# A post-norm block with differential attention and routed experts: a table of two places per step, statistics among a batch's projections, and routed up products turned round

## The chip, the core and the metric

The kernel runs on one core of a Trainium2 chip. The core has five engines that work side by side and meet at semaphores: TensorE (PE, with its weight loads shown apart as PEld), VectorE (DVE), ScalarE (ACT), GpSimd (POOL) and SyncE (SP, which here only issues DMAs). The metric is the device time of one execution in microseconds, lower is better.

## What is computed

The input is four sequences (batches) of 512 tokens of 256 values. Two layers follow each other, each added to its input and normed:

```python
x = _layernorm(x + _L0_attn_ref(x, ...), axis=-1)
x = _layernorm(x + _L0_ffn_ref(x, ...), axis=-1)
```

The attention has 16 heads over 4 key/value groups, each with two score maps under a causal mask; the second softmax is subtracted from the first with a factor lambda. Its output goes through a group norm over a whole batch and is projected:

```python
a1 = _softmax(s1); a2 = _softmax(s2)
diff = a1 - lam * a2
out = jnp.einsum('bhts,bhsd->bhtd', diff, v).transpose(0, 2, 1, 3)
mean = jnp.mean(out, axis=(1, 3), keepdims=True)
var = jnp.var(out, axis=(1, 3), keepdims=True)
out = (out - mean) * jax.lax.rsqrt(var + EPS)
...
return out @ Wo
```

The feed-forward layer picks one of 8 experts for each token (top 1, sigmoid gate), and adds a shared expert:

```python
h = _silu_mul(xs @ wg)      # 256 -> 2 x 512
o = h @ wd                  # 512 -> 256
```

## The kernel before

All of it is written by hand for each engine; the order of instructions on an engine is the order of the code, and semaphores (`wait_ge`) join the engines.

**Attention steps.** A batch b is worked in `body(b, ...)` through 40 steps, the list `STEPS` of (qt, g, kt): 128 queries of tile qt, group g, 128 keys kt. PE writes the scores of a step into a ring of three PSUM banks (`scores`, L950), ACT takes their exponentials (L1178), POOL masks the step where kt equals qt (L1317, 16 such steps a batch: steps 0, 1, 2, 3, 5, 7, 9, 11, 14 and so on), and PE multiplies them with the values one step later (`weigh`, L964). After the last step of a unit (one qt and g) ACT copies the sums out (L1196), PE turns them (task `norm`, L881) and DVE divides and combines them (L1430 to L1433). Beside that PE works "banks" of scores (`score_bank`, L803 and L804) from which DVE takes each row's maximum (L1405); task `mt` turns the finished maxima (L877), and SP carries them into the rows that later scores read.

**The next batch is prepared inside the running one.** `prep` on PE turns x (L787) and projects it into q and k (L791), ACT copies the products out (L1088). POOL then rotates and splits them into three bf16 parts, 18 operations a batch in the list `PREP` (lines 538 to 547), with two casts a pair on ACT (L1102, L1105). `PREP_LATER` (batch 0: `PREP_FIRST`) names the step at which POOL issues each. SP stores the parts and loads them back in stacked form.

**The layer behind attention** for batch b runs among the steps of batch b + 1, as tasks. `TASKS[n]` lists what each engine does at the end of step n; ACT and POOL do them one step later in their own order, behind that step's exponentials or mask. Group norm has the tasks `mean`, `square`, `sum_squares`, `var`; each of four token tiles then has `turn`, `project`, `x2`, `retake`, `logits` (steps 6 + 5 qt on); routing has `top`, `choose`, `gate`, `rank`, `ids`; the shared expert has twelve tasks in steps 28 to 39. `BOUNDARY` stands between two batches: values (`v`, L873), the last `norm` and `sum`. The 8 `prep` of the next batch come at the start of `body`. For the last batch there is nothing to prepare, and what follows its attention is `TAIL`.

**Routed experts.** Tokens are sorted by expert into 23 tiles of 128 rows (`NROUTE`). For each, POOL gathers rows by an indirect DMA, PE turns them (L1026), multiplies with the expert's up weights (L1042: tokens are the stationary side, 512 columns of weights stream, four products), ACT and DVE make the hidden rows, PE turns those (`turn_hidden`, L1050, four 128 by 128 transposes) and ACT copies them (L1251), and PE multiplies with the down weights (L1061). All eight experts' weights (1.5 MB each) lie in SBUF, loaded from body 3 on (`load_experts`), and the expert of a tile selects an address by a register (`owner_of`, L1031).

## Time and profile before

| | us |
|---|---|
| median of 3 runs | 854.79 |
| lowest, highest | 852.37, 856.72 |
| profiled execution, its own time | 854.18 |
| its span, first to last instruction | 852.4 |
| PE busy in the span | 755.7 |
| DVE, ACT, POOL busy | 463.6, 330.5, 305.2 |

The span differs from the profiled execution's own time by 1.8 us at its two ends. The trace gives each instruction's start from the start of the span, its duration, and the idle time of its engine ahead of it with what ended it. Batch 0 has its steps from 73 us, batch 1 its boundary from 190.5, batch 2 from 360.1, batch 3 from 532.7, `TAIL` begins at 638.5, the routed tiles at 703. An instruction's end on PE is modelled and includes the time until its result is out, so groups of matmuls are better read by the distance of their starts.

### The profile page before, as it was taken

The numbers are of one execution on the slowest core, as the hardware profiler recorded it, in microseconds if no ns is written. First come the engines' busy times: TensorE is split into PE (matmuls) and PEld (weight loads), VectorE is DVE, ScalarE is ACT, GpSimd is POOL, SyncE is SP. The second block draws the span as 40 slices with busy tenths as digits, with TensorE's granted clock in tenths as the row PEclk, the third lists the DMA queues.
The fourth block names the chain that finished last, engine by engine and source line by source line (L and its number), as shares of the span: only waits on it lengthen the run. The fifth ranks groups of instructions, "written<-read, shape, count | busy, mean of one in ns | idle before, by whom it ended". The sixth has DMA issues, their size and how long they took to land.

```text
span 852.4 us, 10350 instructions
## 1 busy us (share of the span) xinstructions
PE 755.7 (89%) x3430; PEld 369.7 (43%) x3430; DVE 463.6 (54%) x1040; ACT 330.5 (39%) x607; POOL 305.2 (36%) x263
## 2 busy tenths in 40 slices
PE   7488899997699989977999899889999799999994
PEld 3243334333244433532444334434326555666662
DVE  2766986751667775416677655566425342333332
ACT  2414544434465433154554232554663002222220
POOL 3057511122982012029821130221240034666653
PEclk9778999999899999996899899999999999999998
DMA  3695085002038210020272100700067012221100
GB/s 128 149 335 149 5 197 88 28 2 38 0 70 178 41 55 3 22 42 1 63 161 41 55 4 2 210 2 1 2 207 293 25 44 63 60 60 62 46 22 1
DMA packets 51748, 62.95 MB, mean 74 GB/s; under 512 B 11303, under 2 KB 42797, under 8 KB 49840
## 3 DMA queue, kind: packets, MB, share of 16 engines
q1 hardware_dynamic: 42992, 49.29, 23.4%
q0 software_dynamic: 3824, 6.83, 2.7%
q10 hardware_dynamic: 4880, 6.16, 2.3%
q8 instruction: 29, 0.48, 0.2%
q14 instruction: 23, 0.19, 0.1%
HBM read 42.59 MB, written 22.41 MB: 76 GB/s over the span
## 4 chain that ended last, share of the span: by engine, by line
PE 71%; DVE 10%; POOL 6%; issue 4%; DMA 4%; ACT 2%; SPq 1%; POOLq 0%; DVEq 0%; ACTq 0%
PE pv_ps L964 15%; PE wide_ps L1042 9%; PE wide_ps L950 7%; PE s_ps L803 7%; PE wide_ps L791 5%; DVE mneg L1405 4%; PE wide_ps L934 4%; PE s_ps L835 3%; PE wide_ps L906 3%; PE s_ps L804 3%; PE pv_ps L1061 2%; PE misc L1061 2%; PE misc L881 2%; DMA k_parts<-w_exp 2%; PE wide_ps L939 2%
## 5 line engine op out<-in xcount | busy, mean ns | idle before, releaser
L1405 DVE TENSOR_REDUCE mneg<-s_ps 128x1 f32<-128x384 f32 (+3 forms) x352 | 216.7, 638 | 98.9 <-PE s_ps L804 94.9
L1178 ACT ACTIVATE w_exp<-wide_ps 128x512 f32<-128x512 f32 x320 | 180.0, 599 | 120.6 <-PE wide_ps L950 118.8
L964 PE MATMUL pv_ps<-w_exp,work 128*64 128x512 f32 x640 | 180.5, 644 | 10.0 <-POOL w_exp L1317 8.0
L1317 POOL TENSOR_SCALAR_AFFINE_SELECT w_exp<-w_exp 128x1024 f32<-128x1024 f32 x64 | 70.8, 1106 | 287.1 <-ACT w_exp L1178 287.1
L803 PE MATMUL s_ps<-w_exp 96*128 96x256 bf16 (+3 forms) x512 | 131.6, 316 | 20.7 <-DVE mneg L1405 13.2
L950 PE MATMUL wide_ps<-w_exp 98*128 98x512 bf16 x320 | 124.5, 398 | 13.2 <-ACT w_exp L1178 11.9
L950 PEld LDWEIGHTS wide_ps<-w_exp 98*128 98x128 bf16 x320 | 31.9, 103 | 155.5 <-ACT w_exp L1178 98.4
L804 PE MATMUL s_ps<-mask,identb 128*128 128x128 bf16 (+2 forms) x352 | 89.6, 254 | 0.0
L1042 PE MATMUL wide_ps<-w_exp,tables 128*128 x184 | 82.8, 592 | 0.0
L803 PEld LDWEIGHTS s_ps<-w_exp 96*128 96x128 bf16 x512 | 46.2, 101 | 70.9 <-DVE mneg L1405 43.0
L1196 ACT COPY work<-pv_ps 128x512 f32<-128x512 f32 x64 | 37.5, 585 | 58.1 <-PE pv_ps L964 57.2
L964 PEld LDWEIGHTS pv_ps<-w_exp,work 128*64 128x64 f32 x640 | 32.7, 138 | 54.3 <-issue 37.3
L791 PE MATMUL wide_ps<-work,tables 128*128 128x512 f32 x96 | 49.9, 677 | 6.9 <-ACT work L1088 6.9
L1623 DVE TENSOR_TENSOR work<-work,wide_ps 128x512 f32<-128x512 f32 x23 | 15.8, 688 | 70.8 <-PE wide_ps L1042 70.8
L1042 PEld LDWEIGHTS wide_ps<-w_exp,tables 128*128 128x128 f32 x184 | 33.2, 190 | 33.0 <-issue 33.0
L804 PEld LDWEIGHTS s_ps<-mask,identb 128*128 128x128 bf16 x352 | 36.0, 102 | 22.7 <-issue 4.1
L881 PE MATMUL misc<-ident,work 128*128 128x128 f32 x256 | 40.8, 284 | 2.8 <-ACT work L1158 2.0
L1251 ACT COPY work<-s_ps 128x512 f32<-128x512 f32 x23 | 13.5, 585 | 74.9 <-PE s_ps L1050 68.9
L1430 DVE RECIPROCAL rl<-misc 128x8 f32<-128x8 f32 x64 | 12.8, 200 | 50.5 <-PE misc L881 50.5
L1370 POOL DMA_INDIRECT out<-work,rows_of x23 | 23.6, 1024 | 40.5 <-DVE work L1631 38.5
L1297 POOL TENSOR_TENSOR rstd<-mv,halfneg 128x1 f32<-128x1 f32 x16 | 9.0, 562 | 80.7 <-DVE mv L1471 80.7
L934 PE MATMUL wide_ps<-x2T,w_sh 128*128 128x512 f32 x64 | 34.3, 663 | 1.4 <-DVE place L1534 1.4
(164 smaller groups left out, 982.5 us busy)
## 6 DMA issues: line engine op xcount, KB each, us to landing
w_exp<-q_parts SPq DMA_DIRECT2D x96, 128.0 KB, 5.0
w_exp<-w_up_in SPq DMA_DIRECT2D x8, 1024.0 KB, 8.9
slot_tokens<-x ACTq DMA_DIRECT2D x1, 4864.0 KB, 20.8
work<-x_in SPq DMA_DIRECT2D x8, 512.0 KB, 7.2
w_exp<-w_down_in SPq DMA_DIRECT2D x8, 512.0 KB, 9.6
q_parts<-w_exp SPq DMA_DIRECT2D x6, 512.0 KB, 6.0
w_exp<-k_parts SPq DMA_DIRECT2D x18, 128.0 KB, 3.7
gated_rows<-work SPq DMA_DIRECT2D x4, 512.0 KB
```

Of the source, the lines that this page charges most:

```text
L791: last = nc.tensor.matmul(slot, wqk_sb[:, c, pair, half, :], xT[:, c, :], start=(c == 0), stop=(c == DC - 1))
L803: nc.tensor.matmul(o[:, n], q_stack[0:KROWS, qt, hs, :], keys[0:KROWS, hs // 4, 0:qt + 1, :], start=(n == 0), stop=False)
L804: last = nc.tensor.matmul(o[:, :, w - P:w], identb[:], mask[:].unsqueeze(1).to_broadcast([P, len(rows), P]), start=False, stop=True)
L881: last = nc.tensor.transpose(here[:, r * P:(r + 1) * P], ol[:, arg % 2, r * P:(r + 1) * P], ident[:])
L934: last = nc.tensor.matmul(here[:], w_sh[:, ch * 2 * F + at:ch * 2 * F + at + P], x2T[:, ch, :], start=(ch == 0), stop=(ch == DC - 1))
L950: nc.tensor.matmul(st_bank(v), k_stack[0:MROWS, b % 2, gs, kt, :], q_stack[0:MROWS, qt, gs * 4:gs * 4 + 4, :], start=True, stop=True).then ...
L964: last = nc.tensor.matmul(pv_ps[s * 64:(s + 1) * 64, :], vo[:, kt, g, :], probs[:, n % NP, s, :], start=(kt == 0), stop=(kt == qt))
L1042: last = nc.tensor.matmul(up_ps[:, r, half, :], xeT[:, r, ch, :], w, start=(ch == 0), stop=(ch == DC - 1))
L1178: nc.scalar.activation(probs[:, n % NP, s], st_bank(v), ACT.Exp, scale=float(DH) ** -0.5).then_inc(st_done, 1)
L1196: nc.scalar.copy(ol[:, u % 2], pv_ps[:]).then_inc(pv_done, 1)
L1317: nc.gpsimd.affine_select(out=e, in_=e, compare_op=ALU.is_ge, fill=0.0, base=0, pattern=[[0, 8], [1, P]], channel_multiplier=-1).then_inc( ...
L1405: nc.vector.tensor_reduce(out=mneg[:, qt, rows[0]:rows[-1] + 1], in_=s_ps[:, (v - 1) % 2, 0:len(rows) * w].rearrange("p (r k) -> p r k", r ...
```

## The change

1. **Two places per step.** `TASKS[n]` becomes `TASKS[n, half]`. A task at MID stands on PE between the two halves of a step's banks, ahead of `weigh(n - 1)`; on DVE between the halves; on ACT and POOL it comes in its own step n, behind the exponentials or mask, and no longer one step later. The table is written out anew, place by place: the first tile's `turn` stands at step 3 (before: 6), the second tile's tasks at steps 9 to 12 (before: 11 to 15), routing at 22 to 26 (27 and 28), the shared expert at 25 to 38 (28 to 39). `var`'s ACT part becomes a task `scale` in two halves, `square` too.
2. **The front of a batch.** The 8 `prep` move from the start of `body` into `BOUNDARY`, and `mean`, `square` and the `sum_squares` stand among them. Batch 3 has no `prep`; its boundary keeps the statistics. POOL's `PREP_LATER` and `PREP_FIRST` move to later steps; `bank_table` is spread a little differently.
3. **Routed tiles.** The up product's sides are exchanged: weights are stationary (sixteen products of 128 by 128 by 128 a tile), the tokens stream, and the result is the hidden matrix already turned. `turn_hidden`, `hid`, ACT's `take_hidden` and two semaphores go; DVE writes `hidT` directly.
4. **A ring for up weights.** Only the eight down matrices (0.5 MB each) stay in SBUF. The up weights (1 MB) are loaded for each of the 23 tiles into a ring of four, by SP, which reads the tile's owner into a register; slot i is loaded when `up(i - 4)` is done. POOL gathers the rows of tiles 2 and 3 ahead of the rows to be added.

```diff
-    here = [(2, 0, 8), (3, 8, 19)] if first else [(3, 3, 19)]
-    for back, rows in ((0, here), (-1, [(0, 19, 22), (1, 22, 28), (2, 28, 40)])):
+    here = [(2, 0, 9), (3, 9, 18)] if first else [(3, 2, 20)]
+    for back, rows in ((0, here), (-1, [(0, 20, 22), (1, 22, 28), (2, 28, 39)])):
...
-TASKS[0].append(("mean", 0, 1))
-TASKS[4].append(("var", 0, 1))
...
+put(1, END, ("var", 0, 1))
+put(3, END, ("norm", 1, 0), ("scale", 0, 1), ("scale", 1, 1), ("turn", 0, 1))
+put(9, MID, ("turn", 1, 1))
+put(9, END, ("project", 1, 1))
...
-BOUNDARY = [("v", 0, 0), ("norm", NUNIT - 1, 1), ("sum", QT - 1, 1)]
+BOUNDARY = [("v", 0, 0), ("prep", 0, 0), ("prep", 1, 0), ("norm", 15, 1), ("prep", 2, 0), ("prep", 3, 0), ("sum", 3, 1), ("mean", 0, 1),
+            ("prep", 4, 0), ("square", 0, 1), ("sum_squares", 0, 1), ("sum_squares", 1, 1), ("prep", 5, 0), ("square", 1, 1), ("prep", 6, 0), ("prep", 7, 0), ("sum_squares", 2, 1), ("sum_squares", 3, 1)]
...
-PREP_FIRST = [-4, -4, -3, -3, -2, -1, -1, -1, 0, 1, 2, 3, 3, 4, 4, 5, 6, 7]
-PREP_LATER = [0, 0, 1, 1, 2, 3, 3, 4, 4, 5, 6, 6, 7, 8, 8, 9, 10, 11]
+PREP_FIRST = [-4, -4, -3, -3, -2, -1, -1, -1, 1, 2, 2, 4, 5, 6, 6, 7, 8, 8]
+PREP_LATER = [1, 3, 3, 3, 4, 5, 5, 6, 6, 7, 7, 7, 9, 10, 10, 11, 13, 14]
...
+            def load_upper(i):
+
+                if i >= RINGUP:
+                    sp.wait_ge(up_full, 2 * (i - RINGUP + 1))
+                e = sp.value_load(owner[0:1, i:i + 1], min_val=0, max_val=E - 1)
+                sp.dma_start(w_upper[:, i % RINGUP], w_up.rearrange("e k n -> (e k) n")[bass.ds(e * D, D)].rearrange("(c p) n -> p c n", p=P)
+                             ).then_inc(upper_loaded[i % RINGUP], 16)
...
                 for half in range(2):
-                    for ch in range(DC):
-                        w = w_exp[:, bass.ds(e * WEXP + ch * 2 * F + half * F, F)]
-                        last = nc.tensor.matmul(up_ps[:, r, half, :], xeT[:, r, ch, :], w, start=(ch == 0), stop=(ch == DC - 1))
+                    for fc in range(F // P):
+                        for ch in range(DC):
+                            w = w_upper[:, i % RINGUP, ch, half * F + fc * P:half * F + (fc + 1) * P]
+                            last = nc.tensor.matmul(up_ps[:, r, half, fc * P:(fc + 1) * P], w, xeT[:, r, ch, :], start=(ch == 0), stop=(ch == DC - 1))
                     last.then_inc(up_full, 1)
```

Three places of the order of instructions follow. The first is POOL (GpSimd) at the front of batch 1. L1317 is the mask of a diagonal step; L538, L540, L542, L544, L546, L547 are cos, sin, even, odd, rest and low of a pair; in the changed kernel the lines are L1348 for the mask, L578 to L587 for the six, L1324 and L1325 for the group norm's scale and L1328 for a tile's deviation. Before:

```order
L538 TENSOR_TENSOR work<-w_exp,tables 128x1024
L540 TENSOR_TENSOR rot_sin<-w_exp,tables 128x1024
L1317 AFFINE_SELECT w_exp<-w_exp 128x1024
L542 TENSOR_TENSOR w_exp<-work,rot_sin 128x512
L544 TENSOR_TENSOR w_exp<-rot_sin,work 128x512
L1317 AFFINE_SELECT w_exp<-w_exp 128x1024
L538 TENSOR_TENSOR work<-w_exp,tables 128x1024
L1317 AFFINE_SELECT w_exp<-w_exp 128x1024
L540 TENSOR_TENSOR rot_sin<-w_exp,tables 128x1024
L546 TENSOR_TENSOR w_exp<-w_exp 128x1024
L542 TENSOR_TENSOR w_exp<-work,rot_sin 128x512
L544 TENSOR_TENSOR w_exp<-rot_sin,work 128x512
```

The row ahead of these is batch 1's first mask. Now, from the same mask on:

```order
L1348 AFFINE_SELECT w_exp<-w_exp 128x1024 x3
L578 TENSOR_TENSOR work<-w_exp,tables 128x1024
L1348 AFFINE_SELECT w_exp<-w_exp 128x1024
L1324 TENSOR_TENSOR head_scale<-head_var,halfneg 128x4
L1325 TENSOR_TENSOR head_scale<-head_scale,gw 128x4
L1348 AFFINE_SELECT w_exp<-w_exp 128x1024
L580 TENSOR_TENSOR rot_sin<-w_exp,tables 128x1024
L582 TENSOR_TENSOR w_exp<-work,rot_sin 128x512
L584 TENSOR_TENSOR w_exp<-rot_sin,work 128x512
L578 TENSOR_TENSOR work<-w_exp,tables 128x1024
L1348 AFFINE_SELECT w_exp<-w_exp 128x1024
L1328 TENSOR_TENSOR rstd<-mv,halfneg 128x1
```

The four masks of steps 0 to 3 stood between pairs of preparation; now one preparation and the scale stand between them, and the rest comes behind.

The second is PE (TensorE) at the boundary of batch 1: values (L873, now L926), preparation (L787 and L791, now L840 and L844), `norm` (L881, now L934), `mean` (L890, now L943), `var` (L894, now L947), scores (L950, now L1003). Before:

```order
L873 MATMUL misc<-wv_sb,work 128x128 x8
L881 MATMUL misc<-ident,work 128x128 x4
L787 MATMUL wide_ps<-ident,work 128x128 x8
L791 MATMUL wide_ps<-work,tables 128x512 x12
L950 MATMUL wide_ps<-w_exp 128x512 x5
L890 MATMUL wide_ps<-head_tot,averager 128x16 x4
L950 MATMUL wide_ps<-w_exp 128x512
L964 MATMUL pv_ps<-w_exp,work 64x512 x2
```

Now:

```order
L926 MATMUL misc<-wv_sb,work 128x128 x8
L840 MATMUL wide_ps<-ident,work 128x128 x8
L934 MATMUL misc<-ident,work 128x128 x4
L844 MATMUL wide_ps<-work,tables 128x512 x4
L943 MATMUL wide_ps<-head_tot,averager 128x16 x4
L844 MATMUL wide_ps<-work,tables 128x512 x8
L1003 MATMUL wide_ps<-w_exp 128x512 x6
L1017 MATMUL pv_ps<-w_exp,work 64x512 x2
L1003 MATMUL wide_ps<-w_exp 128x512
L947 MATMUL wide_ps<-averager,work 128x1 x4
```

`mean` has moved from behind the first five scores to the middle of the projections, and `var` from step 4 to step 1.

The third is PE in a routed tile, from the register load of its owner (L1031, now L1084) on: hidden rows turned (L1050), gathered rows turned (L1026, now L1079), up products (L1042, now L1097), down products (L1061, now L1108). Before:

```order
L1031 TENSOR_LOAD tables
L1031 ISA x2
L1050 MATMUL s_ps<-ident,work 128x128 x4
L1026 MATMUL s_ps<-ident,work 128x128 x2
L1042 ISA
L1042 MATMUL wide_ps<-w_exp,tables 128x512
L1042 ISA
L1042 MATMUL wide_ps<-w_exp,tables 128x512
```

Now:

```order
L1084 TENSOR_LOAD tables
L1084 ISA x2
L1079 MATMUL s_ps<-ident,work 128x128 x2
L1097 MATMUL wide_ps<-tables,w_exp 128x128 x16
L1108 ISA
L1108 MATMUL pv_ps<-w_exp,work 128x256
```

The four transposes are gone, sixteen short products stand for four long ones, and no address is worked out for them.

## Rows read from the trace of the kernel before

**Rows 1.** Stages: busy us (count) of PE, PEld, DVE, ACT, POOL; clock, DMA share, GB/s:

```profile
206.50:256.00 49.50, 38.16 (x178) 16.38 (x178) 29.38 (x57) 29.03 (x53) 44.52 (x29) 0.90 0.14 32
376.00:428.00 52.00, 41.56 (x182) 17.09 (x182) 32.49 (x58) 29.78 (x54) 44.58 (x29) 0.80 0.13 31
482.00:532.70 50.70, 49.52 (x203) 21.73 (x202) 25.34 (x55) 14.54 (x26) 9.53 (x8) 0.94 0.06 17
```

**Rows 2.** Timeline, POOL, front of batch 1: start, us, engine, line, what [idle before]:

```profile
207.78 1.09 POOL L1317 TENSOR_SCALAR_AFFINE_SELECT w_exp<-w_exp 128x1024 f32<-128x1024 f32 x1 [21.51 <-ACT w_exp L1178]
...
244.41 0.54 POOL L1297 TENSOR_TENSOR rstd<-mv,halfneg 128x1 f32<-128x1 f32 x1 [3.51 <-DVE mv L1471]
...
252.75 1.09 POOL L1317 TENSOR_SCALAR_AFFINE_SELECT w_exp<-w_exp 128x1024 f32<-128x1024 f32 x1
```

**Rows 3.** Timeline, POOL, front of batch 2: its first and its eighth mask:

```profile
377.39 1.09 POOL L1317 TENSOR_SCALAR_AFFINE_SELECT w_exp<-w_exp 128x1024 f32<-128x1024 f32 x1 [24.68 <-ACT w_exp L1178]
...
424.12 1.08 POOL L1317 TENSOR_SCALAR_AFFINE_SELECT w_exp<-w_exp 128x1024 f32<-128x1024 f32 x1
```

**Rows 4.** Groups by line and shape: count, busy us, mean ns, idle us before:

```profile
L546 POOL TENSOR_TENSOR w_exp<-w_exp 128x1024 f32<-128x1024 f32 x9 | 19.3, 2146 | 0.4 <-ACT w_exp L1102 0.4
L547 POOL TENSOR_TENSOR w_exp<-w_exp 128x1024 bf16<-128x1024 f32 x9 | 19.4, 2160 | 1.5 <-ACT w_exp L1105 1.2
...
L1042 PEld LDWEIGHTS wide_ps<-w_exp,tables 128*128 128x128 f32 x184 | 33.2, 190 | 33.0 <-issue 33.0
```

**Rows 5.** Timeline, PE, batch 1: its waits for maxima, gate and routing:

```profile
288.95 0.23 PE L877 MATMUL misc<-identb,msplit 128*128 128x128 bf16 x1 [0.92 <-DVE o L1431]
...
309.00 0.34 PE L803 MATMUL s_ps<-w_exp 96*128 96x384 bf16 x1 [2.16 <-DVE mneg L1405]
...
310.27 1.14 PE L934 MATMUL wide_ps<-x2T,w_sh 128*128 128x512 f32 x1 [0.73 <-DVE place L1534]
...
357.13 0.22 PE L877 MATMUL misc<-identb,msplit 128*128 128x128 bf16 x1 [1.18 <-DVE msplit L1412]
```

**Rows 6.** Timeline, front of batch 3: statistics and two waits of PE:

```profile
538.00 1.04 PE L890 MATMUL wide_ps<-head_tot,averager 128*128 128x16 f32 x8 [0.17 <-DVE head_tot L1438]
...
539.07 2.61 DVE L1443 TENSOR_TENSOR work<-work,wide_ps 128x512 f32<-128x512 f32 x4 [1.22 <-PE wide_ps L890]
...
541.77 2.19 ACT L1121 ACTIVATE work<-work 128x512 f32<-128x512 f32 x4 [0.87 <-DVEq L1449]
...
544.50 0.39 PE L950 MATMUL wide_ps<-w_exp 98*128 98x512 bf16 x1 [1.61 <-ACT w_exp L1178]
...
558.39 0.39 PE L950 MATMUL wide_ps<-w_exp 98*128 98x512 bf16 x1 [2.36 <-ACT w_exp L1178]
```

**Rows 7.** The chain that ended last, in one routed tile: start, us, what:

```profile
721.59 0.44 PE s_ps L1050 x4
722.02 0.22 PE s_ps L1026 x2
722.24 3.43 PE wide_ps L1042 x8
725.67 1.73 PE pv_ps L1061 x8
```

**Rows 8.** Timeline: the eight 128x128x128 products of `v`, batch 1, and their loads:

```profile
190.45 2.05 PE L873 MATMUL misc<-wv_sb,work 128*128 128x128 f32 x16
190.45 1.86 PEld L873 LDWEIGHTS misc<-wv_sb,work 128*128 128x128 f32 x16 [0.81 <-DVE mT L1425]
```

**Rows 9.** Timeline, PE: its first instruction among the routed tiles:

```profile
703.80 0.43 PE L1026 MATMUL s_ps<-ident,work 128*128 128x128 f32 x2 [1.52 <-issue]
```

**Rows 10.** Stages as in rows 1: while experts load, and among routed tiles:

```profile
641.00:656.00 15.00, 15.00 (x60) 8.42 (x59) 7.93 (x15) 7.19 (x15) 1.25 (x2) 1.00 1.04 384
730.00:780.00 50.00, 50.00 (x192) 31.63 (x191) 18.82 (x51) 12.06 (x25) 31.09 (x35) 1.00 0.20 60
```

**Rows 11.** DMA issues by line: count, KB of one, median us to landing:

```profile
w_exp<-w_up_in SPq DMA_DIRECT2D x8, 1024.0 KB, 8.9
```

More of the change, by code:

```diff
@@ new lines @@
+put(23, MID, ("choose", 0, 1))
+put(24, MID, ("mt", 0, -1))
+put(24, END, ("rank", 0, 1), ("ids", 0, 1))
+put(25, MID, ("shared_gate", 0, 1), ("ids", 1, 1))
+put(25, END, ("norm", 11, 0), ("shared_up", 0, 1))
+put(26, MID, ("gate", 0, 1))
+put(26, END, ("sum", 2, 0))
+put(27, MID, ("shared_gate", 1, 1))
+put(27, END, ("shared_up", 1, 1))
+put(29, MID, ("mt", 1, -1), ("shared_gate", 2, 1))
+put(29, END, ("norm", 12, 0), ("ids", 2, 1))
+put(30, MID, ("ids", 3, 1))
+put(31, MID, ("shared_up", 2, 1))
```

214 lines of the change are left out of this document (111 added, 103 removed).

## The prediction

> **What bounds the kernel now.** I read the stages first, then on each engine the timeline of those where PE is not full, and last the chain. PE is busy for 755.7 of the span's 852.4 us, so a gain comes from three sources only: gaps of PE, time at a lower clock, and PE work itself. The longest gaps lie at the front of batches 1 and 2 [rows 1]: in 206.5 to 256 PE is busy 38.2 of 49.5 us and POOL 44.5, in 376 to 428 PE 41.6 of 52 and POOL 44.6, at a granted clock of 0.90 and 0.80 (a mean of stretches at 2.4 and at 1.2 GHz). POOL sets the pace there: each diagonal step needs its mask from POOL before `weigh`, and POOL reaches the mask only after the preparation queued ahead. From the first mask to the eighth (step 11) POOL takes 252.75 - 207.78 = 44.97 us in batch 1 [rows 2], with one wait of 3.51 for the first tile's variance, and 46.73 in batch 2 [rows 3]. Behind that PE is nearly full, but for waits on DVE [rows 5]. Among the routed tiles PE has no gap: a tile is 0.44 + 0.22 + 3.43 + 1.73 = 5.82 us [rows 7], 23 tiles are 134.
>
> **Batch fronts, POOL's queue.** Now 17 of the 18 preparations stand ahead of the eighth mask; in the change 15 do, since low of pair 1 (step 11), rest and low of pair 2 (13 and 14) come behind it, and only the last was behind it before. That takes out one rest and one low, 2.15 + 2.16 = 4.3 us [rows 4]. The wait of 3.5 should go, since `project` of the first tile stands at step 4 and POOL asks for its variance only in step 5, behind cos of pair 1. The second tile's power is added (0.54) [rows 2]; the scale's two operations are ahead of it in both. The loop through ACT (odd, cast, rest, cast, low) leaves a step or more between each pair of them, so I see no new wait of POOL that is long. Gain: 4.3 + 3.5 - 0.5 = **7.3**, of which my walk through the four early masks gives back 0.3, as mask 1 waits for step 1's exponentials: **7.0** in batch 1. Batch 2 spends 1.8 more over the same queue (46.7 against 45.0), from late statistics, and these now come early: 7.0 + 1.6 = **8.6**. It is only gained if ACT and PE deliver the exponentials in time: in that stage PE's work of 38 us would have to fit in some 41, so the cover is thin.
>
> **Work moved into that stage.** The second tile's `project` (as long as L1061, 1.73 [rows 7]) and `retake` (two transposes, 0.22) now stand ahead of step 12's `weigh`, where PE waits anyway. 2.0 a batch: **4.0**. `mean` goes the other way, into the projections (1.0 us of PE), but PE now has values, a wait for ACT and the projections in an order that hides `norm` 15 behind preparation's transposes, which I set equal. ACT's squares (2.2 us) fit between its copies.
>
> **Waits further on.** In batch 1 these are 0.92 (maxima, `mt` 0), 2.16 (maxima queued on DVE behind routing and gate), 0.73 (`rank`) and 1.18 (`mt` 2), together 5.0 [rows 5]; batch 2 has the same four within 0.05 each. The new table puts `mt` 0 and 2 a step half or more behind their last bank and spreads top, choose, rank and gate over steps 22 to 26. I leave 0.5: 4.5 a batch, **9.0**. In the last third of batch 2 the clock is 0.94 of full [rows 1], 50.7 x 0.06 = 3.0 us lost; without such gaps ahead of it most comes back: **2.5**. A table with more places also makes waits of its own, which no row shows: a MID task stands ahead of `weigh` and of the next score, so whatever it waits for holds both. Between nothing and the 5.0 a batch that it takes away I put 1.5 a batch, nearer to nothing because each chain of a tile has a full step between its links: **+3.0**.
>
> **Batch 0.** It loses two `mt` waits of about 1 us, as in [rows 5], and gets one back (`mt` 2 of batch 0 now follows its last bank in the same step); low of pair 2 stands before the mask of step 9 and waits for a cast that ACT makes after step 9's exponentials, some 1 to 2 us. I take **0**, from -2 to +3.
>
> **Batch 3** has no projections to hide the statistics behind. `mean` starts at 538.0 when DVE's sum is there, in both; but the five scores ahead of it now come later, and ACT must do the squares before the first exponential: 539.07 + 2.61 for the deviations, then 2.19 of squares [rows 6] is 543.9, where before six exponentials were done. PE waits about 1.9 ahead of `mean` and 4.9 behind it, where it had 1.61; the 2.36 for the scale [rows 6] goes, since the variance comes three steps earlier. 1.9 + 4.9 - 1.6 - 2.4 = 2.8, less smaller waits of that stage: **+2.0**.
>
> **Routed tiles.** The transposes of the hidden rows go: -0.44. The up product keeps its streaming: 16 products of 128 columns are as many columns as 4 of 512. What may grow is the distance of starts. Products of this very shape stand in `v`: 16 halves (each float32 product is recorded as two) whose loads start (1.86 - 0.19)/15 = 0.111 us apart [rows 8]; by the matmuls' own row (2.05 - 0.28)/15 = 0.118, with the first, slow one in it. 32 halves at 0.1115 are 3.57 against 3.43, at 0.118 3.78. I take 3.57: the tile is 3.57 + 1.73 + 0.22 = 5.52, and 23 x 0.29 = 6.7. The first turn waits 1.52 for a register load among others [rows 9]; that load now comes later, behind other work: 0.9. Together **7.6**, between 2.8 (0.118) and 8.
>
> The Trainium skill speaks against this ("TensorE: Matmul & The Clock Gate", Part 3, The mechanism): it says that a weight load overlaps a running matmul only when the two use different row groups, and here all use all rows. By that rule loads would stand in line with the streams, the second rival below. In [rows 8] sixteen loads of one row group pass in 1.86 us beside 2.05 us of matmuls, so the trace does not bear it out; the same page's Part 2 (LDWEIGHTS) gives 128/1.2 = 107 ns a load, near the 0.111 seen.
>
> **The ring.** 1 MB a tile is 1.05 MB in 5.52 us, 190 GB/s, beside gathers of 60 GB/s that stretch little; 250 in all. While experts load the core moves 384 GB/s with PE full and undisturbed [rows 10]. The first load is issued when owners are known, more than 10 us ahead of PE's first need, the others up to three tiles ahead. Cost 0. SP's register reads and the small loads of row numbers now queue behind 1 MB loads, 2.7 us each at 384 GB/s; gathers have two tiles of slack.
>
> **Sum.** Against the profiled execution: 854.2 - 7.0 - 8.6 - 4.0 - 9.0 - 2.5 + 3.0 + 0 + 2.0 - 7.6 = **820.5**. The median of before is 0.6 above that execution, which I neglect.
>
> **Rivals.**
> - *The front does not move.* Masks come no earlier because ACT's casts and exponentials wait on each other and PE cannot deliver: the 15.6 and 4.0 stay away: 840. For it: PE's 38 us in 41; ACT's cast of a pair stands in order ahead of the next exponentials. Against: ACT is busy 29 of 49.5 us.
> - *Weight loads exposed.* Each half costs its load of 0.190 [rows 4] beyond its stream of 0.107 (3.43/32): 9.5 against 3.57, 23 x 5.9 = +137: 957. It cancels the whole sum from 33.7/23 = 1.5 us a tile on, 0.046 a half.
> - *The ring starves PE* (slower). A 1 MB load took 8.9 us to land [rows 11]. If loads came one after another at that pace, the tile is 8.9: 23 x 3.4 = +78: 898. It decides from 5.52 + 33.7/23 = 7.0 us a tile. For it: 23 MB where 8 were, one queue with the row numbers. Against: those 8.9 us were with others in flight, at 384 GB/s together [rows 10].
> - *Better than summed*: no new waits, the clock stays up in the fronts too: 5 to 12 less, 812.
>
> **Chances.** Forecast 0.55 (its own range 813 to 829), front unmoved or half moved 0.24, better 0.12, ring 0.06, loads 0.03. The first three reach from 808 to 842; that holds 8 in 10. About 0.5% (4.3 us) is what a measurement can tell from no change: faster 0.89, within 0.02 (the far end of the second case), slower 0.09, all of it from the ring and the loads.
>
> **What would show it.** The eighth mask of batch 1 38 us after the first (now 45), of batch 2 the same; no wait over 0.5 us before `mt` and the shared expert; batch 3's front with one gap of about 5 us ahead of its second group of scores; starts of the up halves 0.11 apart and a tile of 5.5 us; the DMA at about 250 GB/s among the tiles. It is wrong if PE waits for `upper_loaded` or for gathered rows, if POOL waits for casts, or if DVE, which now has the second tile's tasks among the banks of the last query tile, becomes what PE waits for.

## The result, and the profile after

The changed kernel takes **825.39 us** (median of 4 runs, 822.43 to 826.78) where the kernel before takes 853.58 beside it; the ratio is 0.967 (95% interval 0.9635 to 0.9711). The forecast was 820.5, range 808 to 842. So 28.2 us of the 33.7 that were summed did come. The profiled execution has a span of 825.1 us, 27.3 below that of the kernel before.

The page of the changed kernel begins so (busy time of each engine; among the lines on 40 slices the granted clock of PE):

```profile
PE 740.3 (90%) x3890; PEld 407.1 (49%) x3890; DVE 471.5 (57%) x1040; ACT 316.6 (38%) x584; POOL 308.1 (37%) x263
...
PEclk9878999999989999999999998799999999999997
```

To see where the time went, cut both traces at the same pieces of work: `v` of each batch (the boundary's first product), the first product of the last shared expert's tail, the first turn among the routed tiles, the end of the last down product. In us:

| stage | before | after | difference | forecast |
|---|---|---|---|---|
| head, to batch 0's `v` | 20.99 | 20.48 | -0.5 | 0 |
| batch 0 | 169.46 | 167.92 | -1.5 | 0 |
| batch 1 | 169.62 | 158.74 | -10.9 | -12.0 |
| batch 2 | 172.58 | 158.42 | -14.2 | -16.1 |
| batch 3, to the tail's start | 106.38 | 110.90 | +4.5 | +2.0 |
| tail, to the first routed turn | 64.77 | 66.01 | +1.2 | -0.9 |
| routed tiles, to the last product's end | 137.10 | 129.86 | -7.2 | -6.7 |
| what follows it | 11.5 | 12.7 | +1.2 | 0 |
| span | 852.4 | 825.1 | -27.3 | -33.7 |

(The forecast of batch 1 is 7.0 + 2.0 + 4.5 less half of the 3.0 for new waits, of batch 2 8.6 + 2.0 + 4.5 + 2.5 less the other half.)

**Fronts.** Timeline of POOL in batch 1: its first two masks (of steps 0 and 1), the second tile's deviation (rstd), the eighth mask, and low of pair 2:

```profile
205.34 2.14 POOL L1348 TENSOR_SCALAR_AFFINE_SELECT w_exp<-w_exp 128x1024 f32<-128x1024 f32 x2 [19.79 <-ACT w_exp L1216]
...
242.47 0.55 POOL L1328 TENSOR_TENSOR rstd<-mv,halfneg 128x1 f32<-128x1 f32 x1 [2.33 <-DVE mv L1501]
...
245.47 1.15 POOL L1348 TENSOR_SCALAR_AFFINE_SELECT w_exp<-w_exp 128x1024 f32<-128x1024 f32 x1
...
256.33 2.13 POOL L587 TENSOR_TENSOR w_exp<-w_exp 128x1024 bf16<-128x1024 f32 x1 [3.39 <-ACT w_exp L1149]
```

(In the order of instructions above, the three masks ahead of cos are these two and the last one of batch 0.) The eighth mask comes 245.47 - 205.34 = 40.1 us after the first, where it was 45.0 [rows 2]; the forecast was 38. The difference is about the wait of 2.33 for the second tile's variance, which the forecast had at nothing. That wait is not fixed: with the same order of instructions it is absent in the traces of e6 and e9 below, where the eighth mask comes 37.74 us after the first, while e12 has 40.86. In batch 2 it is 39.05 (46.73 before, [rows 3]). PE's longest wait in the front of batch 1, for a mask, has nearly gone. Before, and now:

```profile
214.60 1.81 PE L964 MATMUL pv_ps<-w_exp,work 128*64 128x512 f32 x4 [3.97 <-POOL w_exp L1317]
```

```profile
206.49 1.08 PE L1017 MATMUL pv_ps<-w_exp,work 128*64 128x512 f32 x4 [0.37 <-POOL w_exp L1348]
```

The stages of [rows 1] read now (PE, PEld, DVE, ACT, POOL busy; clock, DMA share, GB/s):

```profile
204.00:254.00 50.00, 41.07 (x201) 18.58 (x202) 30.40 (x57) 28.39 (x52) 43.93 (x30) 0.93 0.13 28
362.50:412.50 50.00, 41.66 (x204) 19.01 (x203) 30.87 (x57) 28.63 (x52) 43.87 (x30) 0.93 0.14 30
455.00:505.50 50.50, 49.87 (x234) 22.51 (x231) 31.78 (x66) 17.20 (x31) 9.61 (x7) 1.00 0.08 24
```

PE has more to do per us than before (41.1 of 50 where it was 38.2 of 49.5), and batch 2's last third is at full clock, where it was at 0.94. Of PE's remaining waits in batch 1, the two longest and the last:

```profile
228.28 0.61 PE L1003 MATMUL wide_ps<-w_exp 98*128 98x512 bf16 x1 [3.45 <-ACT w_exp L1216]
...
245.82 0.41 PE L964 MATMUL wide_ps<-ident,x 128*128 128x128 f32 x2 [2.11 <-DVE x L1506]
...
276.90 0.40 PE L856 MATMUL s_ps<-w_exp 96*128 96x128 bf16 x4 [0.63 <-DVE mneg L1435]
```

The third is the last one of the batch over 0.3 us: the four waits of [rows 5], 5.0 us, are gone from batches 1 and 2. The first two belong to the front, as do one of 1.34 and one of 0.71.

**Batch 3.** Timeline of its front, PE, DVE and ACT:

```profile
510.90 1.86 PE L943 MATMUL wide_ps<-head_tot,averager 128*128 128x16 f32 x8 [1.96 <-DVE head_tot L1468]
...
512.80 2.60 DVE L1473 TENSOR_TENSOR work<-work,wide_ps 128x512 f32<-128x512 f32 x4 [2.04 <-PE wide_ps L943]
...
515.49 2.19 ACT L1165 ACTIVATE work<-work 128x512 f32<-128x512 f32 x4 [7.26 <-DVEq L1479]
...
518.22 1.58 PE L1003 MATMUL wide_ps<-w_exp 98*128 98x512 bf16 x3 [4.18 <-ACT w_exp L1216]
519.96 1.97 PE L1017 MATMUL pv_ps<-w_exp,work 128*64 128x512 f32 x4 [0.16 <-POOL w_exp L1348]
```

PE waits 1.96 ahead of `mean` and 4.18 behind it, 6.1 where [rows 6] has 0.17 + 1.61 + 2.36 = 4.1: the 2.0 of the forecast. What is not in it is the clock: `mean` takes 1.86 where it took 1.04 [rows 6], and four halves of `weigh` 1.97 where they take 1.08 at 2.4 GHz (from 528.88 on). The granted clock is 0.50 from 510.96 to 528.0, 17.1 us; before it fell, PE had waited 0.68 and 1.96 us. In the kernel before, batch 3 has two stretches of 3.4 us at that level.

**Routed tiles.** PE at their start, and a tile of the chain that ended last (start, us, what):

```profile
682.47 0.41 PE L1079 MATMUL s_ps<-ident,work 128*128 128x128 f32 x2 [1.66 <-DMA work<-gated_rows,rows_of]
683.43 0.41 PE L1079 MATMUL s_ps<-ident,work 128*128 128x128 f32 x2 [0.55 <-ACT tables L1277]
683.68 3.74 PE L1097 MATMUL wide_ps<-tables,w_exp 128*128 128x128 f32 x32
689.15 0.44 PE L1079 MATMUL s_ps<-ident,work 128*128 128x128 f32 x2 [1.73 <-DMA work<-gated_rows,rows_of]
```

```profile
722.49 0.22 PE s_ps L1079 x2
722.71 3.57 PE wide_ps L1097 x32
726.28 1.73 PE pv_ps L1108 x8
```

A tile is 0.22 + 3.57 + 1.73 = 5.52, as summed, against the 5.82 of [rows 7]; 32 halves take 3.57 at 0.1116 apart. The first turn waits about as long as in [rows 9], now for gathered rows and not for a register. The third waits 1.73, since its gather could start only when the first turn had freed one of the two buffers. Stage 730 to 780, to be held against the second of [rows 10], and the ring's loads:

```profile
730.00:780.00 50.00, 50.00 (x384) 47.70 (x383) 19.79 (x54) 8.99 (x19) 33.49 (x37) 1.00 0.73 252
```

```profile
w_exp<-w_up_in SPq DMA_DIRECT2D x23, 1024.0 KB, 5.5
```

252 GB/s, and PE waits for no load of the ring.

**The end** is 1.2 us longer because the last two down products now follow each other directly; the last one used to wait 0.76 us for a copy by ACT, behind the transposes. The last two tiles' results therefore reach DVE and POOL together. POOL's last power of -0.5 waits for the scatter of the tile ahead:

```profile
810.44 1.89 PE L1108 MATMUL pv_ps<-w_exp,work 128*128 x8
...
812.94 0.42 DVE L1673 TENSOR_TENSOR work<-pv_ps,work 128x256 f32<-128x256 f32 x1
...
813.87 1.04 POOL L1400 DMA_INDIRECT out<-work,rows_of  x1 [1.29 <-DVE work L1666]
...
814.94 0.57 POOL L1395 TENSOR_TENSOR out_rstd<-out_mv,halfneg 128x1 f32<-128x1 f32 x1
...
816.78 1.03 POOL L1400 DMA_INDIRECT out<-work,rows_of  x1 [1.26 <-DVE work L1666]
```

From the product's end (812.33) to the start of the last scatter are 4.45 us; before, 3.24.

### The profile page after: what moved, and what is told of

Same layout as the page of the kernel before. It is cut to its first block, busy times and chain, and to the rows that moved or that the text cites. A ratio compares the mean times of both kernels' runs of the same rounds, so it can differ in the third digit from the quotient of the medians.

```text
span 825.1 us, 11250 instructions
## 1 busy us (share of the span) xinstructions
PE 740.3 (90%) x3890; PEld 407.1 (49%) x3890; DVE 471.5 (57%) x1040; ACT 316.6 (38%) x584; POOL 308.1 (37%) x263
## 4 chain that ended last, share of the span: by engine, by line
PE 69%; DVE 13%; POOL 6%; issue 5%; DMA 3%; ACT 2%; SPq 1%; POOLq 0%; DVEq 0%; ACTq 0%
PE pv_ps L1017 16%; PE wide_ps L1097 10%; PE s_ps L856 7%; PE wide_ps L1003 7%; DVE mneg L1435 6%; PE wide_ps L844 5%; PE wide_ps L987 3%; PE s_ps L888 3%; PE s_ps L857 3%; PE wide_ps L959 3%; PE misc L1108 2%; PE pv_ps L1108 2%; PE misc L934 2%; POOL w_exp L1348 2%; PE wide_ps L992 2%
## 5 line engine op out<-in xcount | busy, mean ns | idle before, releaser
L1017 PE MATMUL pv_ps<-w_exp,work 128*64 128x512 f32 x640 | 176.7, 633 | 3.0 <-ACT work L1234 1.9
L1348 POOL TENSOR_SCALAR_AFFINE_SELECT w_exp<-w_exp 128x1024 f32<-128x1024 f32 x64 | 70.7, 1108 | 278.8 <-ACT w_exp L1216 278.8
L856 PE MATMUL s_ps<-w_exp 96*128 96x256 bf16 (+3 forms) x512 | 129.9, 313 | 17.5 <-DVE mneg L1435 9.4
L1003 PE MATMUL wide_ps<-w_exp 98*128 98x512 bf16 x320 | 122.4, 397 | 15.4 <-ACT w_exp L1216 14.0
L1003 PEld LDWEIGHTS wide_ps<-w_exp 98*128 98x128 bf16 x320 | 31.0, 102 | 154.0 <-ACT w_exp L1216 83.3
L1097 PE MATMUL wide_ps<-tables,w_exp 128*128 128x128 f32 x736 | 85.9, 275 | 0.0
L1097 PEld LDWEIGHTS wide_ps<-tables,w_exp 128*128 128x128 f32 x736 | 84.1, 192 | 0.1
L844 PE MATMUL wide_ps<-work,tables 128*128 128x512 f32 x96 | 49.8, 672 | 6.1 <-ACT work L1132 6.1
L1658 DVE TENSOR_TENSOR work<-work,wide_ps 128x512 f32<-128x512 f32 x23 | 15.8, 689 | 64.8 <-PE wide_ps L1097 64.8
L857 PEld LDWEIGHTS s_ps<-mask,identb 128*128 128x128 bf16 x352 | 35.6, 101 | 21.6 <-issue 2.2
L934 PE MATMUL misc<-ident,work 128*128 128x128 f32 x256 | 40.1, 281 | 1.5 <-ACT work L1234 0.8
L1277 ACT COPY tables<-s_ps 128x256 f32<-128x256 f32 x23 | 8.6, 373 | 77.9 <-PE s_ps L1079 77.9
L578 POOL TENSOR_TENSOR work<-w_exp,tables 128x1024 f32<-128x1024 f32 x9 | 21.1, 2349 | 36.5 <-ACT w_exp L1132 36.2
L844 PEld LDWEIGHTS wide_ps<-work,tables 128*128 128x128 f32 x96 | 19.9, 216 | 29.5 <-issue 21.7
L1328 POOL TENSOR_TENSOR rstd<-mv,halfneg 128x1 f32<-128x1 f32 x16 | 9.1, 568 | 67.8 <-DVE mv L1501 67.8
```

Of the source, the lines that this page charges most:

```text
L844: last = nc.tensor.matmul(slot, wqk_sb[:, c, pair, half, :], xT[:, c, :], start=(c == 0), stop=(c == DC - 1))
L856: nc.tensor.matmul(o[:, n], q_stack[0:KROWS, qt, hs, :], keys[0:KROWS, hs // 4, 0:qt + 1, :], start=(n == 0), stop=False)
L857: last = nc.tensor.matmul(o[:, :, w - P:w], identb[:], mask[:].unsqueeze(1).to_broadcast([P, len(rows), P]), start=False, stop=True)
L934: last = nc.tensor.transpose(here[:, r * P:(r + 1) * P], ol[:, arg % 2, r * P:(r + 1) * P], ident[:])
L1003: nc.tensor.matmul(st_bank(v), k_stack[0:MROWS, b % 2, gs, kt, :], q_stack[0:MROWS, qt, gs * 4:gs * 4 + 4, :], start=True, stop=True).then ...
L1017: last = nc.tensor.matmul(pv_ps[s * 64:(s + 1) * 64, :], vo[:, kt, g, :], probs[:, n % NP, s, :], start=(kt == 0), stop=(kt == qt))
```

## Experiments

All runs are compared with the kernel before on the same chip: e1 to e4 on one, e5 to e8 on a second, e9 to e12 on a third. The stages, cut as above (us), are of one trace each, and the rows "before" and "after" are the two traces of the section above. The head, 20.2 to 21.3 us, is left out:

| kernel | batch 0 | batch 1 | batch 2 | batch 3 | tail | tiles | end | span | ratio (95%) |
|---|---|---|---|---|---|---|---|---|---|
| before | 169.5 | 169.6 | 172.6 | 106.4 | 64.8 | 137.1 | 11.5 | 852.4 | |
| after | 167.9 | 158.7 | 158.4 | 110.9 | 66.0 | 129.9 | 12.7 | 825.1 | 0.967 (0.9635, 0.9711) |
| e1, routed part alone | 169.4 | 169.4 | 172.4 | 106.7 | 64.9 | 130.3 | 12.7 | 846.1 | 0.991 (0.9878, 0.994) |
| e2, table and fronts alone | 167.9 | 158.8 | 158.5 | 110.8 | 65.9 | 137.1 | 11.5 | 831.4 | 0.973 (0.9703, 0.9757) |
| e3, batch 3's statistics late | 167.6 | 158.7 | 158.4 | 107.4 | 66.7 | 129.5 | 12.7 | 821.4 | 0.963 (0.9603, 0.966) |
| e4, POOL's list of before | 167.1 | 164.2 | 164.2 | 109.9 | 65.5 | 130.2 | 12.7 | 834.3 | 0.983 (0.9783, 0.9868) |
| e5, POOL's list later | 168.8 | 169.3 | 167.3 | 110.8 | 65.6 | 131.9 | 12.7 | 847.7 | 0.993 (0.9905, 0.9958) |
| e6, ring loaded twice | 168.2 | 156.4 | 158.4 | 110.4 | 68.2 | 141.3 | 12.7 | 836.7 | 0.984 (0.9818, 0.9868) |
| e7, straight product, ring | 166.9 | 158.3 | 158.5 | 111.0 | 66.7 | 137.2 | 11.5 | 830.3 | 0.976 (0.974, 0.9786) |
| e8, start of the routed part | 167.8 | 158.7 | 158.4 | 110.8 | 65.0 | 127.9 | 12.7 | 822.0 | 0.965 (0.9622, 0.9672) |
| e9, e3 and e8 | 167.9 | 156.4 | 158.4 | 107.4 | 65.1 | 128.3 | 12.7 | 816.9 | 0.960 (0.9557, 0.9635) |
| e10, e9 and second tile | 168.0 | 158.5 | 158.5 | 106.7 | 66.8 | 129.3 | 12.7 | 821.2 | 0.959 (0.9555, 0.9625) |
| e11, e10 and `mt` | 166.4 | 158.8 | 158.5 | 107.2 | 66.7 | 127.9 | 12.7 | 818.8 | 0.958 (0.9543, 0.9618) |
| e12, after, once more | 167.7 | 160.2 | 158.8 | 111.0 | 66.7 | 130.1 | 12.7 | 827.5 | 0.965 (0.9626, 0.9682) |

### The two halves of the change (e1, e2)

e1 is the kernel before with parts 3 and 4 of the change (products turned, ring, order of gathers), e2 the kernel before with parts 1 and 2.

> The routed part alone (ring for the up weights, turned up products, order of gathers), with the table, boundary and preparation of the kernel before. The two traces put the routed tiles 7.2 us shorter (137.1 to 129.9 from the first turn to the last product) and the end 1.3 longer. Theory A, the parts add up: span 852.4 - 7.2 + 1.3 = 846.5, a ratio of 0.993, a tile at 5.5 us between starts, and the first turn waits for its gathered rows as in the changed kernel, 1 to 2 us. Theory B, the ring costs where the experts' loads of before did not and the fronts hid it: over 850, with waits for upper_loaded or gathered rows in the middle of the tiles.

> The table, the boundary and the later preparation alone, routed tiles as before. By the stages of the two traces the attention part gives 0.5 + 1.5 + 10.9 + 14.2 - 4.5 = 22.6 us up to the tail. Theory A, the parts add up: span 852.4 - 22.6 = 829.8 give or take 1.5, a ratio of 0.974, routed tiles at 5.82 us, and batch 3 as long as in the changed kernel, 110.9 us. Theory B: batch 3's 4.5 us more come from the down weights that are loaded in one piece of seven experts at its start; then batch 3 is near 106.4 here, and the span near 825.

Both came as theory A has them: 846.1 (846.5 expected) and 831.4 (829.8 give or take 1.5; it is 0.1 outside, and the expectation had left out that the tail is 1.1 longer). The two halves lie in different stages and add up: -6.3 and -21.0 make the -27.3 of the whole. The loads of down weights that the change puts into batch 3 play no part: e2 loads the experts as the kernel before does, and its batch 3 is 110.8.

### Batch 3 (e3)

The edit, in short (task, then step and place in the table):

```diff
 for batch 3 only:
-BOUNDARY: v, norm 15, sum 3, mean, square 0, sum_squares 0, 1, square 1, sum_squares 2, 3
-var (1, END), scale (3, END), turn 0 (3, END), project 0 (4, END), x2 0 (5, END), retake 0 (7, MID), logits 0 (8, MID)
+BOUNDARY: v, norm 15, sum 3
+mean (0, END), square 0, 1 (1, END), sum_squares 0, 1 (2, END), 2, 3 (3, END), var, scale (4, END)
+turn 0 (5, END), project 0 (6, END), x2 0 (7, END), retake 0 (8, MID), logits 0 (8, END)
```

> The changed kernel, but in batch 3 alone mean, squares, sums and variance stand behind steps 0 to 4 again, the first tile's tasks in steps 5 to 8 and none in the boundary. Theory A: batch 3 became 4.5 us longer because its boundary has no projections over which the statistics can run, so PE waits 2.0 and 4.2 us there and the clock falls to 1.2 GHz for what follows (the scores' products at 519.96 took 0.49 each). Then batch 3 returns to 106 to 107 us, the gap of 4.2 goes, and the span is 825.1 - 4.5 = 820.6 (ratio 0.9625). Theory B, the tighter table of steps 3 to 12 is what costs in batch 3: it stays at 110 to 111 and the waits only move into steps 5 to 12: 825.

Batch 3 fell to 107.4, span 821.4 (820.6 expected). So where the statistics stand is the cause. The gap of 4.18 is gone, and so is most of the stretch at 1.2 GHz. The first 40 us from `v` on, in before, after and e3, in that order:

```profile
532.65:572.65 40.00, 33.59 (x168) 16.04 (x168) 24.41 (x53) 21.15 (x41) 9.34 (x10) 0.91 0.40 112
```

```profile
505.56:545.56 40.00, 32.86 (x156) 16.41 (x155) 23.73 (x49) 19.65 (x38) 9.65 (x10) 0.79 0.47 126
```

```profile
504.95:544.95 40.00, 33.04 (x173) 16.84 (x172) 24.23 (x52) 21.55 (x42) 9.62 (x10) 0.96 0.47 126
```

PE's busy time is nearly the same in all three, while what it got done in it is 168, 156 and 173 instructions. The whole batch, in the same order:

```profile
532.65:639.03 106.38, 98.16 (x484) 41.46 (x483) 56.24 (x136) 61.40 (x116) 27.17 (x27) 0.97 0.27 84
```

```profile
505.56:616.46 110.90, 100.84 (x485) 42.80 (x483) 59.02 (x136) 61.10 (x116) 28.42 (x27) 0.92 0.22 62
```

```profile
504.95:612.35 107.40, 97.56 (x484) 41.38 (x483) 57.71 (x136) 60.68 (x116) 28.35 (x27) 0.98 0.23 64
```

PE is idle for 8.2, 10.1 and 9.8 us of it. Of the 4.5 us that the change added, 1.8 are idle time and 2.7 are longer busy time at the lower clock. e3 takes back hardly any idle time (its waits are shorter and more of them) and 3.3 us of busy time; its stretch at 1.2 GHz is 3.4 us instead of 17.1. All seven traces of the changed boundary other than e4's (the changed kernel twice, e2, e5 to e8) have one stretch of about 17 us; e4's is 13.7. This is theory A, and the division between waits and clock is an account of PE's time, not a run of its own. Time at 1.2 GHz is not lost one for one either: e10 has the boundary of e3 and 10.3 us at that level, and its batch 3 is 106.7, with PE idle for 6.4.

### POOL's queue (e4, e5)

```diff
-PREP_LATER = [1, 3, 3, 3, 4, 5, 5, 6, 6, 7, 7, 7, 9, 10, 10, 11, 13, 14]
+PREP_LATER = [0, 0, 1, 1, 2, 3, 3, 4, 4, 5, 6, 6, 7, 8, 8, 9, 10, 11]        (e4)
+PREP_LATER = [1, 3, 4, 5, 5, 6, 7, 8, 8, 9, 10, 10, 12, 12, 13, 14, 15, 16]   (e5)
```

> The changed kernel with one list undone: GpSimd's preparation stands at the steps of before (0, 0, 1, 1, 2, 3, 3, 4, 4, 5, 6, 6, 7, 8, 8, 9, 10, 11). Theory A, GpSimd's queue sets the fronts: the eighth mask of batch 1 comes 44 to 45 us after the first instead of 40.1, since two preparations more stand ahead of it (4.3 us), each of batches 1 and 2 is 4 to 6 us longer, and the span is 825.1 + 10 = 835 (ratio 0.979). Theory B, the fronts got shorter because statistics and prep were merged into the boundary, and the masks follow PE and ACT: within 2 us of 825.

> The changed kernel with GpSimd's preparation moved further back: steps 1, 3, 4, 5, 5, 6, 7, 8, 8, 9, 10, 10, 12, 12, 13, 14, 15, 16, so that two preparations more (low of pair 1 is behind the eighth mask already; now its rest, and odd or even of pair 2) come behind the eighth mask of a batch. Theory A, GpSimd's queue still sets the front: 40.1 us from the first mask to the eighth becomes 36 to 37, PE's waits of 3.45 and 2.11 us in batch 1 shrink, and the span falls by 2 x 3 us to 819. Theory B, the front is by now PE's own (41.4 of 50 us busy) and what GpSimd no longer does there it does later in front of other masks, or the parts come late for the next batch's banks: within 1.5 us of 825 or slower.

e4 came as theory A has it: first and eighth mask of batch 1 stand 248.36 - 204.56 = 43.8 us apart,

```profile
204.56 1.09 POOL L1348 TENSOR_SCALAR_AFFINE_SELECT w_exp<-w_exp 128x1024 f32<-128x1024 f32 x1 [19.80 <-ACT w_exp L1216]
...
248.36 1.15 POOL L1348 TENSOR_SCALAR_AFFINE_SELECT w_exp<-w_exp 128x1024 f32<-128x1024 f32 x1
```

and batches 1 and 2 are 5.5 and 5.8 longer, the span 9.3. Two operations of 2.15 us each stand ahead of the eighth mask again, and at 211.36 PE waits 2.95 us for a mask. Taking this list away costs 11.3 of the 25.0 us that these two batches had gained; the other 13.7 stay, with the table and the boundary. (One trace each; e12 below shows how far such a figure can be trusted.)

e5 is a miss of theory A; of theory B, the slower end came. In its trace 12 preparations stand ahead of the eighth mask, three fewer than the 15 of the change (the expectation counted two), and that gives nothing (40.4 us to the eighth mask) and costs 10.5 and 8.9 us a batch. Two rows say why. The stage of batch 1's front, and PE's first bank of scores for the next batch:

```profile
206.00:256.00 50.00, 42.15 (x192) 18.89 (x194) 30.75 (x56) 26.43 (x49) 38.74 (x27) 0.86 0.04 11
```

```profile
283.20 0.60 PE L856 MATMUL s_ps<-w_exp 96*128 96x128 bf16 x4 [5.96 <-DMA w_exp<-q_parts]
```

POOL has room (38.7 of 50 busy where it was 43.9), yet PE is no faster: its clock is 0.86, its wait ahead of `retake` is 4.03 where it was 2.11, and POOL now waits for exponentials and variances (2.94, 2.37, 1.77, 3.72 us). And low of pair 2 ends at 269.5 instead of 258.5, so that the stacked parts of the next batch reach PE 5.96 us late. That wait recurs in batch 2 (5.79) and stands in neither batch of the changed kernel. The list of the change lies between these two: a shorter queue of POOL helps only as long as the other engines can go on, and the other end of the same list is a deadline that a DMA chain sets.

### The ring and the turned product (e6, e7)

e6 loads each up matrix a second time into memory that nobody reads. e7 keeps the ring and takes the product, PE's turn of the hidden rows and ACT's copy from the kernel before.

```diff
+                sp.dma_start(w_second[:, i % RINGUP], w_up...[bass.ds(e * D, D)]...).then_inc(upper_loaded[i % RINGUP], 16)     (e6)
...
-                pe.wait_ge(upper_loaded[i % RINGUP], (i // RINGUP + 1) * 16)
+                pe.wait_ge(upper_loaded[i % RINGUP], (i // RINGUP + 1) * 32)
```

> The changed kernel with every up matrix loaded twice, the second time into memory that nobody reads, and up waiting for both: 2 MB a tile where there was 1. Theory A, the ring costs nothing because the queue has room: 2.1 MB at the 419 GB/s that the page shows at most is 5.0 us, below the tile's 5.5, and gathers come on top (0.4 MB): 2.5 MB need about 6.0 us, so the tile grows to 6.0 to 6.3 and the span to 825 + 23 x 0.6 = 839; the limit would then stand at about two loads a tile. Theory B, already one load costs (through gathers and row numbers queued behind it): the tile rises by more than 1.5 us, and the span is over 860. Theory C, no change: 825, bandwidth is not near its limit.

> The changed kernel with the ring kept but the up product as before: tokens stationary, four products of 512 columns, the hidden rows turned by PE and copied by ACT. Theory A: of the 0.32 us that a tile lost (5.82 to 5.5), all comes from the products and transposes and none from the ring, so the tile is 5.8 again and the span 825.1 + 23 x 0.3 = 832 (ratio 0.975). Theory B: the loads of experts that are gone from batch 3 and from the front of the tail made the difference; then the tile stays at 5.5 to 5.6.

e7's tile in the chain (turn of the hidden rows, turn of the tokens, up, down) is that of the kernel before:

```profile
734.37 0.44 PE s_ps L1107 x4
734.80 0.22 PE s_ps L1082 x2
735.02 3.44 PE wide_ps L1099 x8
738.46 1.73 PE pv_ps L1118 x8
```

5.82 us, span 830.3 (832 expected): all of the 0.30 a tile goes with the product and its transposes, and the ring costs nothing there. In e6 the distance of turns stays between 5.52 and 5.65 for eleven tiles, while the ring's lead lasts, and the last eight are 5.93 on average, with waits such as

```profile
788.55 3.84 PE L1101 MATMUL wide_ps<-tables,w_exp 128*128 128x128 f32 x32 [0.70 <-DMA w_exp<-w_up_in]
```

```profile
w_exp<-w_up_in SPq DMA_DIRECT2D x8, 1024.0 KB, 16.5
```

The second row, of the DMA issues in 780 to 820, gives the landing time; from 780 to 812 the slices of that view show about 400 GB/s. Its third and fourth turns come 11.1 and 7.7 us after the ones before them: the row numbers stand behind 2 MB a tile, PE waits 4.50 us for gathered rows, and the up products ahead of that wait and behind it take 6.09 and 5.69 in place of 3.74, at the lower clock. The tiles are 11.5 us longer, the span 11.6 (14 expected), but only 3.3 of that are the last eight tiles; some 7.5 are these two turns at the start. The steady tile of 5.93 also lies below the 6.0 to 6.3 expected. So the point from which the ring would starve PE lies just under twice its traffic: at 400 GB/s a tile of 5.52 us leaves room for 2.2 MB, gathers included.

### The start of the routed part (e8), and a version of both (e9)

```diff
-            load_upper(0)
             sp.wait_ge(tokens_scattered, NTOK * 16)
-            for i in range(2):
+            for i in range(ID_GROUPS[2][1]):
                 load_ids(i)
+            load_upper(0)
...
-        xe = theirs.take(2 * D).rearrange("p (u d) -> p u d", u=2)
+        xe = work[:, 10240:10240 + 4 * D].rearrange("p (u d) -> p u d", u=4)
...
-                if i >= 2:
-                    pool.wait_ge(turned, i - 1)
+                if i >= 4:
+                    pool.wait_ge(turned, i - 3)
```

> The changed kernel with the start of the routed part put right: SP reads the row numbers of tiles 0 to 3 before the first load of the ring, and the gathered rows have four buffers instead of two, so that gathers 2 and 3 need not wait for the first turns. Theory A: the first turn's wait of 1.66 for gathered rows falls below 0.5 and that of the third, 1.73, goes: span 825.1 - 2.5 to 3.3 = 822. Theory B, the first turn waits as long for something else (the register load of 1.52 as in the kernel before, or upper_loaded, since the first load is issued later): 824 to 826.

> The changed kernel with two corrections together: batch 3's statistics behind steps 0 to 4 (its own run took 3.5 us off batch 3) and the start of the routed part (row numbers first, four buffers for gathered rows; its own run took 1.0 off the way to the first turn and 1.9 off the tiles). Theory A, they lie in different stages and add up: span 825.1 - 3.7 - 3.1 = 818.3, and the first turn waits 0.7 us as it does with the second correction alone. Theory B, the row numbers hang on something that does not come earlier with batch 3 (with the first correction alone the first turn's wait grew from 1.66 to 2.37): then 0.7 of it is lost, 819.

The first gather in the changed kernel and in e8 (timeline, POOL):

```profile
675.71 1.05 POOL L1381 DMA_INDIRECT work<-gated_rows,rows_of  x1 [8.35 <-DMA rows_of<-slot_tokens]
```

```profile
672.14 1.05 POOL L1380 DMA_INDIRECT work<-gated_rows,rows_of  x1 [4.98 <-DMA rows_of<-slot_tokens]
```

It starts 3.6 us earlier. The first turn waits 0.67 in place of 1.66, the third not at all; the span is 822.0, as expected. In e9 the first turn waits 0.67 too, and the two corrections add up: span 816.9 (818.3 expected), 819.54 us median of 6 runs (815.78 to 824.82), ratio 0.960, against 825.51 (824.38 to 829.21) and 0.965 for the changed kernel (e12) in the same comparison. It is faster than both kernels. Batch 1 alone, whose code is that of the changed kernel, is 2.4 us shorter in this trace, more than the 1.4 us by which the span lies below the sum.

### Two more edits, and the changed kernel again (e10, e11, e12)

e10 is e9's kernel with the first edits below, e11 is e10's with the last.

```diff
-PREP_LATER = [1, 3, 3, 3, 4, 5, 5, 6, 6, 7, 7, 7, 9, 10, 10, 11, 13, 14]
+PREP_LATER = [1, 3, 3, 3, 4, 5, 5, 6, 6, 7, 7, 7, 9, 9, 9, 11, 13, 14]          (e10, e11)
-put(11, MID, ("retake", 1, 1))
-put(12, END, ("logits", 1, 1))
+put(12, MID, ("retake", 1, 1))
+put(13, MID, ("logits", 1, 1))
...
-put(8, END, ("mt", 2, 0))
-put(9, MID, ("turn", 1, 1))
+put(9, MID, ("mt", 2, 0), ("turn", 1, 1))                                        (e11)
```

> The kernel of the run before, with even and odd of pair 2 taken forward to step 9 on GpSimd, where it waited 2.33 us for the second tile's variance, and the second tile's retake and logits one step later, at the middle of steps 12 and 13. Theory A: GpSimd's wait is filled, the eighth mask comes 2 us earlier, PE's gap of 2.11 ahead of retake goes, 1.5 to 2 us a batch in batches 1 and 2: span 3 to 4 below the run before. Theory B, the front's length is PE's work and the clock: the gap only moves, within 1 us of the run before.

> The kernel of the run before, with the turn of the maxima of query tile 2 in batch 0 half a step later, at the middle of step 9 instead of the end of step 8, where PE waited 1.18 us for it. Theory A: 1 us less in batch 0 (167.9 to 166.9). Theory B: the rows of maxima come later through two DMAs to step 12, and scores wait there instead: no gain or a loss of 1.

> The changed kernel as it is, in the same comparison as the three above: 825.4, a ratio of 0.967. A second trace of it shows how much of a stage's length is chance: all theories expect the starts of batches within 0.3 us of 188.4, 347.1 and 505.6, and if they are off by more, then differences of 1 to 2 us in a batch's front (as between the runs with a doubled ring, 156.4 us for batch 1, and the changed kernel, 158.7, whose code there is the same) are the clock's, not the edit's.

e10 went theory B's way: the gap ahead of `retake` went, others of 3.45 and 0.99 stand ahead of scores, and batch 1 is 158.5 with the eighth mask at 39.5. e11's batch 0 is 1.6 shorter than e10's and the wait of 1.18 is gone, but the medians of e9, e10 and e11, 819.54, 819.43 and 819.29, cannot be told apart.

e12 is what these differences have to be held against. The same code took 158.7 us in batch 1 in one trace and 160.2 in the other, and with other ends of the program (e6, e9) 156.4. The stage 204 to 254 in the changed kernel is shown under "Fronts" (clock 0.93, PE x201); in e12 and e6:

```profile
204.00:254.00 50.00, 43.02 (x194) 19.16 (x193) 30.39 (x56) 27.98 (x51) 43.25 (x30) 0.86 0.12 27
```

```profile
204.00:254.00 50.00, 42.45 (x214) 19.21 (x214) 32.24 (x62) 29.19 (x54) 43.86 (x30) 0.97 0.16 32
```

POOL is equally busy in all three; the clock is 0.93, 0.86 and 0.97, and the instructions that PE got done follow it, 201, 194 and 214. e9, on the chip and in the comparison of e12, has 156.4 as well, so it is not a difference of chips. One batch in one trace is known to no better than 2 us either way.

## Why the prediction was right, and where its terms were off

- **Fronts, POOL's queue** (7.0 and 8.6). Right in mechanism: e4 puts the list alone at 5.5 and 5.8 a batch, PE's wait for a mask comes back with it, and the stretch from the first mask to the eighth fell by 4.8 and 7.7 us. The rival of an unmoved front is out. The forecast of 38 us was met in e6 and e9 (37.74) and missed by 2 to 3 in the changed kernel's own two traces, with waits of POOL for a tile's variance that differ between traces of the same code, as the clock does. e5 bounds this source: a queue shortened further gives nothing. What the sum did not name is how much of this gain would be clock. Over batches 1 and 2 together, PE's idle time fell from 35.6 to 21.5 us, and the time lost at 1.2 GHz (half of its busy time at that level) from 18.0 to 6.5, while the sum had 2.5 for the clock. e4 gives its 11.3 back nearly all on the clock's side (17.3 lost, idle 22.1). Where POOL sets the pace, slow work of PE fills what would else be a wait, so these two figures do not say which is cause.
- **Work moved** (4.0), **later waits** (9.0), **new waits** (+3.0), **clock of batch 2** (2.5). The four waits went, with 0.6 left where 0.5 was put, and batch 2's last third is at full clock. The waits of the table's own are the 2.11 ahead of `retake`, which falls in the front. Together with the fronts, batches 1 and 2 gave 25.0 where 28.1 were summed; the same code gives batch 1 anything from 156.4 to 160.2 us, so these terms cannot be told apart from one another to better than 2 us, nor is the +3.0 for new waits confirmed by itself.
- **Batch 0** (0): it gave 1.5, one of its `mt` waits and shorter fronts; 1.18 us stayed at `mt` 2 of both kinds. Its bounds of -2 to +3 held.
- **Batch 3** (+2.0): the term that failed most, +4.5. The waits were sized right, 2.0 more. What was left out is the clock: 17.1 us at 1.2 GHz, from `mean` through the scores and `weigh` behind it. e3 gives 3.5 of the 4.5 back by moving the statistics, and the granted clock of the first 40 us goes from 0.79 to 0.96. The sum had credited the clock where waits went (batch 2) and had not debited it where they came.
- **Routed tiles** (7.6): the tile was 5.52 as worked out from the distance of `v`'s products, and e7, without the turned product, is back at 5.82. The rival of exposed weight loads is out: 736 halves of products took 85.9 us of busy time beside 84.1 us of loads,

```profile
L1097 PE MATMUL wide_ps<-tables,w_exp 128*128 128x128 f32 x736 | 85.9, 275 | 0.0
...
L1097 PEld LDWEIGHTS wide_ps<-tables,w_exp 128*128 128x128 f32 x736 | 84.1, 192 | 0.1
```

  all on the same 128 rows, at 0.1116 us from start to start (3.57/32). The Trainium skill's sentence ("TensorE: Matmul & The Clock Gate", Part 3, The mechanism), that a load overlaps a running matmul only if their row groups differ, is contradicted by these rows. The 0.9 at the first turn did not come: the register load went, and the gather of rows, until then hidden, stood right behind it with 1.66. The gather waited for row numbers behind the first 1 MB load. e8 took 1.0 off the way to the first turn and 2.0 off the tiles; by the places of the waits the first is the row numbers' and the second the buffers', but the two edits were not run apart.
- **What was not in the sum**: +1.2 at the end, a tile's results queued behind those of the tile ahead, once nothing separates the last two down products (e1 has it, 12.7, e2 and e7, which turn the hidden rows, do not). And +1.2 in the tail, with nearly the same waits as before: there a stretch of 8 us has a clock of 0.79, in before, at the same distance from the tail's start, 1.00 (PE alone; after, then before):

```profile
656.46:664.46 8.00, 7.98 (x23) 0.79 0.25 87
```

```profile
679.03:687.03 8.00, 7.61 (x26) 1.00 0.32 108
```

  The waits of the routing ahead of it are there in both, to 0.02 us. Such a stretch stands in the tail of all twelve traces that have the new table and in neither of the two that have the old one (before, and e1 with 64.9), so it goes with the first half of the change; what in it makes the clock fall stays open.
- **The ring** (0): right, with waits only at the start. The slower rival put the deciding point at 7.0 us a tile from a landing time of 8.9. e6 shows that landing time (16.5 us there, with a tile of 5.9) was no measure of pace, since the loads overlapped; the sum of bytes was, about 400 GB/s.
- **The whole.** Batches 1 and 2, batch 3, the tail and the end came out 3.1, 2.5, 2.1 and 1.2 us above their terms, and head, batch 0 and tiles 0.5, 1.5 and 0.5 below: 6.4 short in all, inside the stated range. Some 4.7 of it is PE's time lost at the lower clock in batch 3 and in the tail, which the sum had not priced; the rest is within what one trace can tell.

## What to carry to other kernels

Cost a wait that you add twice: its own length, and the clock of PE for the work behind it, of which only the part that nothing else covers is lost. A place with no other PE work to fill it (here the last batch's boundary) wants a table of its own. When you take work out of an in-order queue, look for both ends: beyond the point where another engine sets the pace it gains nothing, and the work moved back has a consumer with a deadline. When weights are re-loaded in a ring, put the small transfers that start the pipeline ahead of the first large one.

## What the runs showed of the chip

The same instructions in the same order took 156.4 to 160.2 us a batch in different executions, with a granted clock from 0.97 to 0.86 in the stage above and waits of PE and POOL that shift with it; e6 and e9 differ from the changed kernel only in later stages. Float32 products of 128x128x128 with a new weight load each run at 0.1116 us a half, 4% slower than four products that stream 512 columns (3.57 against 3.43 us for the same work). A queue of 1 MB loads beside indirect gathers moved about 400 GB/s with PE at 5.93 us a tile; at the 252 GB/s of the ring alone PE waited for none of its loads.
